# Turning gathered rows by a DMA on f16 halves instead of on TensorE in f32

## The reference, cut to what matters

```python
xn = _layernorm(x)
x = x + gnn(xn, edge_weight, bias, edge_index) + mix(xn, W_qkv, qn_w, kn_w, W_out, b_out)
x = x + ffn(_layernorm(x), norm_scale, gate_w, gate_b, mlp1_w, mlp1_b, mlp2_w, mlp2_b)
...
def ffn(x, ...):                         # E = 8, K = 2, I = 256
    t = x * rsqrt(mean(x * x) + 1e-5) * norm_scale
    top_v, top_i = top_k(t @ gate_w + gate_b, K)
    w = zeros((T, E)).at[arange(T)[:, None], top_i].set(softmax(top_v))
    for e in range(E):
        h = swiglu(t @ mlp1_w[e] + mlp1_b[e])        # (T, 1024) x (1024, 512) -> (T, 256)
        acc += w[:, e:e+1] * (h @ mlp2_w[e] + mlp2_b[e])
    return x + acc
```

## Time and profile before

| | us |
|---|---|
| median of 3 runs | 1025.75 |
| the profiled execution, its time | 1022.55 |
| the profiled execution, its span | 1020.8 |
| PE busy in the span | 922.0 |
| DVE busy | 708.9 |
| ACT busy | 366.5 |
| POOL busy | 173.5 |

### The profile page before, as it was taken

How to read it: one execution, slowest core, us unless ns; L and a number is a source line. 1 busy time by engine, 2 the same in 40 slices (tenths; PEclk the granted TensorE clock), 3 DMA queues, 4 the chain that set the end, 5 groups by cost and what they waited for, 6 DMA issues and landing times.

```text
span 1020.8 us, 16203 instructions
## 1 busy us (share of the span) xinstructions
PE 922.0 (90%) x5361; PEld 576.2 (56%) x5362; DVE 708.9 (69%) x1198; ACT 366.5 (36%) x621; POOL 173.5 (17%) x210
## 2 busy tenths in 40 slices
PE   3998999999999999998998999998359999999992
PEld 2555667766665654555665666665335455555551
DVE  4867999999999974378856777755455455555551
ACT  5657666666441114431122222222112233333331
POOL 1000000000000000015222223322122233323322
PEclk9999999999999999999999999999569999999997
DMA  9735676666663009910255555566459978886544
GB/s 303 227 92 167 201 221 213 194 195 191 213 199 123 22 22 231 336 53 1 61 163 148 159 161 158 151 175 172 177 197 311 315 185 251 270 252 144 123 83 62
DMA packets 89162, 176.59 MB, mean 173 GB/s; under 512 B 24824, under 2 KB 39160, under 8 KB 89088
## 3 DMA queue, kind: packets, MB, share of 16 engines
q1 hardware_dynamic: 81328, 147.50, 46.1%
q0 software_dynamic: 7776, 28.32, 12.4%
HBM read 113.63 MB, written 62.67 MB: 173 GB/s over the span
## 4 chain that ended last, share of the span: by engine, by line
PE 41%; DVE 20%; DMA 18%; ACT 6%; issue 5%; POOL 4%; SPq 3%; DVEq 1%; POOLq 0%; ACTq 0%
PE bank L758 10%; PE windows L1033 9%; DMA arena<-in_w_flat 7%; PE bank L907 7%; DMA arena<-t_dram,arena 6%; PE bank L1051 4%; DVE arena L1687 2%; POOL arena L655 2%; DMA out_x<-arena 2%; DVE arena L1510 2%; PE bank L1024 2%; SPq L541 2%; DMA arena<-in_w_qkv 2%; PE windows L790 2%; DVE arena L1520 2%
## 5 line engine op out<-in xcount | busy, mean ns | idle before, releaser
L758 PE MATMUL bank<-arena 128*125 128x512 f16 x960 | 217.0, 384 | 10.2 <-DVE arena L1483 10.2
L758 PEld LDWEIGHTS bank<-arena 128*125 128x125 f16 x960 | 130.5, 138 | 84.2 <-issue 11.3
L1033 PE MATMUL windows<-arena 128*128 x648 | 149.5, 381 | 0.0
L907 PE MATMUL bank<-arena 128*128 128x416 f16 (+1 forms) x576 | 105.7, 338 | 2.0 <-DMA arena<-split_dram 2.0
L1033 PEld LDWEIGHTS windows<-arena 128*128 128x128 f16 x648 | 63.7, 98 | 65.6 <-issue 1.4
L933 PE MATMUL bank<-arena 128*125 128x512 f16 x432 | 96.3, 379 | 3.8 <-DVE arena L1723 2.3
L939 PE MATMUL bank<-arena 128*125 128x512 f16 x432 | 97.5, 384 | 0.0
L1749 DVE SCALAR_TENSOR_TENSOR arena<-arena 128x512 f16<-128x512 f32 x40 | 39.3, 982 | 61.8 <-ACT arena L1322 61.8
L907 PEld LDWEIGHTS bank<-arena 128*128 128x128 f16 x576 | 55.0, 97 | 45.5 <-DMA arena<-split_dram 2.4
L933 PEld LDWEIGHTS bank<-arena 128*125 128x125 f16 x432 | 58.7, 137 | 37.8 <-DVE arena L1723 2.7
L939 PEld LDWEIGHTS bank<-arena 128*125 128x125 f16 x432 | 59.7, 138 | 34.3 <-issue 1.6
(11 more groups left out here) (248 smaller groups left out, 1428.1 us busy)
## 6 DMA issues: line engine op xcount, KB each, us to landing
arena<-split_dram SPq DMA_DIRECT2D x56, 512.0 KB, 5.5
arena<-in_w_flat SPq DMA_DIRECT2D x44, 512.0 KB, 4.5
split_dram<-arena SPq DMA_DIRECT2D x88, 256.0 KB, 4.6
arena<-in_w_flat SPq DMA_DIRECT2D x40, 256.0 KB, 4.5
split_dram<-arena SPq DMA_DIRECT2D x80, 128.0 KB, 2.3
arena<-in_x SPq DMA_DIRECT2D x20, 448.0 KB
arena<-in_w_qkv SPq DMA_DIRECT2D x8, 1024.0 KB, 11.7
t_dram<-arena SPq DMA_DIRECT2D x10, 448.0 KB
```

The source lines that it names most:

```text
L758: mm = pe.matmul(bank[b][0:TT, :], xt[:, l, k, tok(i)], wkv[:, r, k, c0:c0 + 512], start=(k == 0 and n == 0), stop=(k == KT - 1 and n == 2))
L907: mm = pe.matmul(bank[u % 3][:, 0:n], wq[h][:, l, k, :], xt[:, r, k, a:a + n], start=(k == 0 and c == 0), stop=(k == KT - 1 and c == 2))
L1033: mm = pe.matmul(bank[6][:, :], rowT[s][:, l, k, :], arena16[:, bass.ds(off + (r * KT + k) * 512, 512)], start=(k == 0 and c == 0), stop=( ...
```

## The change

Where tiles of t are stored, they are stored as two f16 halves, high and low, side by side in a row of 2 x 1024 f16 (as many bytes as 1024 f32). ACT makes the high half (`split_hi`) and DVE the low half (`split_lo`) of each of the 10 tiles. SP stores the halves once the low half is there. `tm` in f32 is still what the gate reads.

In the expert stage a gathered row is then already two f16 halves. ACT issues one transposing DMA a block (`turn`), from `rows[s]` (128 rows of 2048 f16) to `rowT[s]` (128 rows of 16 x 128 f16), both in SBUF. PE's 8 transposes, ACT's two copies and DVE's two subtractions of a block are gone. PE's up product waits for the DMA (`turn_in`); POOL's next gather into the same rows buffer waits for it too, where it waited for PE's transposes.

```diff
-    t_dram = scratch("t_dram", [N, D], F32)
+    t_dram = scratch("t_dram", [N, 2 * D], F16)
...
+        t_hl = [view(tail.at + h * 4 * D, [2, D], F16) for h in range(2)]
...
-        rows = [T2([D]) for _ in range(2)]
+        rows = [T2([2 * D], F16) for _ in range(2)]
...
-        rowT = [T2([2, KT, P], F16) for _ in range(2)]
+        rowT = [T2([2 * KT, P], F16) for _ in range(2)]
...
             def store_mixed(i):
                 h = i % 2
-                sp.wait_ge(t_ready, i + 1)
-                tile_dma(sp, t_rows[i], tm[h], t_out[h])
+                sp.wait_ge(t_lo, i + 1)
+                tile_dma(sp, t_rows[i], t_hl[h].rearrange("p a b -> p (a b)"), t_out[h])
...
             with pool.Fori(1, (BLOCKS - 3) // 2) as t:
                 for h in range(2):
-                    pool.wait_ge(rt_psum, 2 * t + h + 1)
+                    pool.wait_ge(turn_in[h], 16 * (t + 1))
                     gather(2 * t + h + 2, h)
                     add_block(2 * t + h - 2, h)
...
-            def row_T(b, s, q):
-
-                pe.wait_ge(row_in[s], 16 * (q + 1))
-                for k in range(KT):
-                    mm = pe.transpose(bank[2 + 2 * s + k // 4][:, (k % 4) * P:(k % 4 + 1) * P], rows[s][:, k * P:(k + 1) * P], ident)
-                mm.then_inc(rt_psum, 1)
-
-            def up(b, s, off, half):
+            def up(b, s, q, off, half):
                 if half == 0:
-                    pe.wait_ge(rt_done, b + 1)
+                    pe.wait_ge(turn_in[s], 16 * (q + 1))
                     pe.wait_ge(h_evac, b)
...
-                if not last:
-                    row_T(b + 1, 1 - s, q + s)
                 pe.wait_ge(expert_ready, need + 1)
-                up(b, s, off, 0)
+                up(b, s, q, off, 0)
...
+            def split_hi(i):
+                h = i % 2
+                a_.wait_ge(t_ready, i + 1)
+                a_.wait_ge(t_out[h], 32 * (i // 2))
+                a_.activation(t_hl[h][0:TT, 0, :], tm[h][0:TT], ACT.Copy).then_inc(t_hi, 1)
...
             for i in range(NT - 2, NT):
                 mix_sqrt(i - 1, 1 - i % 2)
-                for q in quarters(i):
+                for q in quarters(i, 0, 1):
+                    quarter_split(q)
+                split_hi(i - 1)
+                for q in quarters(i, 1):
                     quarter_split(q)
                 tt_copy(i - 1)
             mix_sqrt(NT - 1, 1)
+            split_hi(NT - 1)
             tt_copy(NT - 1)
...
-            def row_hi(b, s, first=False):
-                a_.wait_ge(rt_psum, b + 1)
+            def turn(b, s, q, first=False):
+
+                a_.wait_ge(row_in[s], 16 * (q + 1))
                 if not first:
                     a_.wait_ge(h_mm, b - 1)
-                for q in range(2):
-                    a_.activation(rowT[s][:, 0, 4 * q:4 * q + 4, :], bank[2 + 2 * s + q][:, :].rearrange("p (k n) -> p k n", n=P), ACT.Copy).then_inc(rt_hi, 1)
+                apart(a_)
+                a_.dma_start_transpose(rowT[s], rows[s]).then_inc(turn_in[s], 16)
...
             with a_.Fori(0, (BLOCKS - 3) // 2) as t:
                 for h in range(2):
                     b = 2 * t + h + 2
-                    row_hi(b + 1, 1 - h)
+                    turn(b + 1, 1 - h, t + 1 + h)
                     act_hi(b - 1)
                     scale_y(b - 2, h)
                     sigmoid(b)
...
+            def split_lo(i):
+                v.wait_ge(t_hi, i + 1)
+                v.tensor_tensor(t_hl[i % 2][0:TT, 1, :], tm[i % 2][0:TT], t_hl[i % 2][0:TT, 0, :], ALU.subtract).then_inc(t_lo, 1)
...
             for i in range(NT - 2, NT):
                 mix_norm(i - 1, (i - 1) // 2, 1 - i % 2)
                 gate(i - 3)
-                for q in quarters(i, 0, 3):
+                for q in quarters(i, 0, 1):
+                    quarter_split(q)
+                split_lo(i - 1)
+                for q in quarters(i, 1, 3):
                     quarter_split(q)
...
             mix_norm(NT - 1, NT // 2 - 1, 1)
+            split_lo(NT - 1)
             gate(NT - 3)
             gate(NT - 2)
             gate(NT - 1)
...
-            def row_lo(b, s):
-                for q in range(2):
-                    v.wait_ge(rt_hi, 2 * b + q + 1)
-                    ins = v.tensor_tensor(rowT[s][:, 1, 4 * q:4 * q + 4, :], bank[2 + 2 * s + q][:, :].rearrange("p (k n) -> p k n", n=P),
-                                          rowT[s][:, 0, 4 * q:4 * q + 4, :], ALU.subtract)
-                ins.then_inc(rt_done, 1)
```

More of the change, by code:

```diff
@@ L167, in build_gps_layer @@
         tail = Place(A_AT + 40000, A_AT + 65536)
+        t_hl = [view(tail.at + h * 4 * D, [2, D], F16) for h in range(2)]
         kvn = tail([PAIRS, P])
         kvt = tail([2, PAIRS * P], F16)
+        assert tail.at == A_AT + 40000 + 8 * D
         head_mask = tail([P])
@@ L298, in build_gps_layer @@
         sd2_ready = sem("sd2_ready"); stat2_ready = sem("stat2_ready")
-        t_ready = sem("t_ready")
+        t_ready = sem("t_ready"); t_hi = sem("t_hi"); t_lo = sem("t_lo")
         t_out = [sem(f"t_out{h}") for h in range(2)]
@@ L307, in build_gps_layer @@
         row_in = [sem(f"row_in{h}") for h in range(2)]; idx_ready = sem("idx_ready")
-        rt_psum = sem("rt_psum"); rt_hi = sem("rt_hi"); rt_done = sem("rt_done")
+        turn_in = [sem(f"turn_in{h}") for h in range(2)]
         h_mm = sem("h_mm"); h_evac = sem("h_evac"); glu_ready = sem("glu_ready"); sg_ready = sem("sg_ready")
@@ L711, in _ @@
             for b in range(2):
-                pool.wait_ge(rt_psum, b + 1)
+                pool.wait_ge(turn_in[b], 16)
                 gather(b + 2, b)
@@ L1053, in down, with expert_block @@
                 mm.then_inc(y_mm, 1)
-            def expert_block(b, s, q, first=False, last=False):
+            def expert_block(b, s, q, first=False):
                 off = pe.value_load(blk_i[0:1, bass.ds(b, 1)], min_val=0, max_val=TOP // 2 - 12288)
                 need = pe.value_load(exp_i[0:1, bass.ds(b, 1)], min_val=0, max_val=E)
-                if not last:
-                    row_T(b + 1, 1 - s, q + s)
                 pe.wait_ge(expert_ready, need + 1)
-                up(b, s, off, 0)
+                up(b, s, q, off, 0)
                 if not first:
                     act_T(b - 1)
-                up(b, s, off, 1)
+                up(b, s, q, off, 1)
                 if not first:
@@ L1068, in _ @@
             pe.wait_ge(count_in, 1)
-            row_T(0, 0, 0)
             expert_block(0, 0, 0, first=True)
@@ L1074, in _ @@
             expert_block(BLOCKS - 2, 1, (BLOCKS - 2) // 2)
-            expert_block(BLOCKS - 1, 0, (BLOCKS - 1) // 2, last=True)
+            expert_block(BLOCKS - 1, 0, (BLOCKS - 1) // 2)
             act_T(BLOCKS - 1)
@@ L1330, in _ @@
                 attend_hi(j, 1, PAIRS + j)
+            split_hi(0)
             tt_copy(0)
@@ L1338, in _ @@
                     quarter_split(qs[j - 1])
+                    if j == 1:
+                        split_hi(i - 1)
                     attend_hi(4 * h + j, t + 1, PAIRS * (t + 1) + 4 * h + j)
@@ L1373, in scale_y @@
                 a_.activation(ysb[s], ysb[s], ACT.Copy, scale=p_of[:, bass.ds(b, 1)]).then_inc(y_scaled, 1)
-            row_hi(0, 0, first=True)
-            row_hi(1, 1, first=True)
+            turn(0, 0, 0, first=True)
+            turn(1, 1, 0, first=True)
             sigmoid(0)
-            row_hi(2, 0)
+            turn(2, 0, 1)
             act_hi(0)
@@ L1761, in _ @@
                 add_half(1, 1, half)
+            split_lo(0)
             for i in range(2, NT - 2):
```

14 lines of the change are left out of this document (5 added, 9 removed).

## The result

The changed kernel takes 1129.99 us, the median of 4 runs (1117.13 to 1138.79), beside 1027.37 us for the kernel before in 4 runs on the same chip. The ratio is 1.091, with a 95% interval of 1.084 to 1.099: about 9% slower, where 1045 us, 1.7% more, had been forecast. The profiled execution of after took 1117.13 us with a span of 1115.4.

What follows compares the result with a forecast made beforehand. PE sets the pace in light stretches, with gathers late beside weights; the changed stage was priced by full DMA engines. 16 + 0.5 + 3.5 + 1 = +21 on 1022.55 gave 1043.5, stated as 1045 us; range 1003 to 1150.

Steps and rivals of the forecast that it cites:

- The last step of the sum: Whole kernel: from 1043.5 us for the profiled execution to 1045 us, the median of the runs standing 3.2 us above it.
- the forecast's own signs: Expert stage: DMA share above 0.9 in light stretches and PE idle at the up product's head would confirm the forecast.
- The free transfer: Rival, expert stage: a turn costs 1.4 us with overlapping packet times, PE's savings come back, about 1004 us; chance 0.22.
- the rival of the scatter chain: Expert stage: each scatter waits for the one before, so PE's gain cannot be used; about 1027 us; chance 0.13.
- The loop of a row buffer: Expert stage: gather, turn, then 2.7 us on POOL; 12.2 us for two blocks alone, 20.2 us beside weights.
- the rival of the long turn: Expert stage: a block turned piece after piece, 20 us long without filling the engines; about 1220 us; chance 0.08.
- The turn's price, 2.3 us a block: Expert stage: DMA engine time for 524 KB at the rate of the graph matrix's 256-byte stores; 62 us for 27 blocks.
- the forecast's formula: Expert stage: engine time over a mean share of 0.93, (197 + 62) giving 279 us against 263, +16 us.
- ACT's 0.4 us: Expert stage: ACT's own cost of issuing a turn, taken from SP's 433 ns for a load of as many bytes.
- The first block: Start of the expert stage: a turn of 5 us moves the first up product from 756.03 to 756.5, +0.5 us.
- The gate of tile 7: End of the mix stage: the last low half stands on DVE ahead of this gate, delaying PE's gate product, +3.5 us.
- SP's store of t: Mix stage: the store waits for the low half, and SP's quarter stores and loads follow; +1 us (0 to 7).

Runs made afterwards that it cites:

- after_no_weights: The changed kernel without the weight loads of experts 3 to 7 (products use the weights of the experts three before): 1082.29 us, ratio 1.060 to the kernel before.
- turn_behind: The changed kernel with ACT issuing the turn behind the copy of the activations and the scaling: 1134.08 us, ratio 1.103 to the kernel before.
- before_plus_turn: The kernel before with one unneeded transposing DMA a block added on ACT's queue: 1152.11 us, ratio 1.106 to the kernel before.
- half a turn: The changed kernel turning only the high halves, the low halves being zero: 1079.38 us, ratio 1.054 to the kernel before.
- the small copy: The changed kernel with each turn replaced by two plain DMAs of the same bytes in 256-byte pieces: 1095.45 us, ratio 1.069 to the kernel before.
- the plain copy: The changed kernel with the turn replaced by a plain DMA of the same 524 KB, not turned: 1055.48 us, ratio 1.030 to the kernel before.
- store_late: The changed kernel with SP's store of t issued behind the quarters and the load of the next tile: 1109.54 us.

## Why the prediction was wrong in size

- *What fell short.* The sum had 1043.5 us for the profiled execution, which took 1117.13. Of the 74 us between, 48 lie in the expert stage (64.3 where 16.5 were forecast) and 26 in the mix stage (30.2 where 4.5 were). The last step of the sum is off by 1.7 us besides (1043.5 and 3.2 make 1046.7, not 1045).
- *Direction and mechanism of the expert stage: right in part.* The engines are full in loaded stretches, the mean share is the 0.93 that was taken, and PE waits at the head of the up product for the turn. In light stretches the forecast's own signs failed: a share above 0.9 was named, two of the three shown have 0.81 and 0.86, and PE is busy for 20.00 and 19.30 of 20 us in them. The free transfer is refuted, and so is the rival of the scatter chain, which had no change: PE waits for turns and for the low half, though POOL also waited longer for the scatter before (64.6 us, 45.5 before).
- *The failed step: the turn's length beside weights.* The loop of a row buffer was worked out with a turn of 5 us alone and 8 beside weights, 10.1 us a block, and then left out of the sum, which went by engine time. Beside weights a turn took 22.52 us in after and 25.29 in `after_no_weights`; with 22.5 the forecast's loop gives (9.5 + 22.5 + 2.7) / 2 = 17.4 us a block. Without weights the range is wide: 4.91 us in `turn_behind`, 5.64 to 10.54 in `after_no_weights`, 17.29 in after. The long transfer is mostly a matter of the pieces, not of the turning: the plain copy in 256-byte pieces took 17.16 us beside weights and 7.32 without. So the rival of the long turn, with a chance of 0.08, came true in part, beside weights; but it had the engines not full, and there they were.
- *The turn's price, 2.3 us a block: too low.* It came from packets of 18.1 ns. A packet of the turn costs 28.3 ns here, and a block 3.68 us: 99 us in all, not 62. The price of the pieces was nearly right: plain 256-byte packets cost 19.5 ns in the turn's place and 20.2 beside the kernel before (6.7% of 1056.2 us). What the stores of the earlier trace rows could not show is the price of turning, 24.2 ns a packet in `after_no_weights` (8.0% of 1063.1 us) and 37.8 in `before_plus_turn`.
- *That full engines alone make the sum: wrong.* With 99 us the forecast's formula, (197 + 99) / 0.93 = 318 us, gives 55 of the 64 us; but a stage's length is its engine time over its share whatever the cause, so this proves little. Where the formula is tested it falls short: half a turn, 44 us of engines (4.1% of 1074.4 us), needs 259 us and took 289.1; the small copy, 68 us, needs 285 and took 309.8 at a share of 0.87; the plain copy, 36 us, needs 250 and took 268.4. The length of the transfer stands in PE's chain.
- *ACT's 0.4 us: wrong.* SP's price for issuing as many bytes held for the plain copy (0.47 us) and not for the turn (1.3 to 11.0 us). The text counted a hold of the whole turn to the upper end only; it is where PE's 35.3 us at the down product come from: with the turn issued behind that copy, 2.3 are left (2.2 before the change).
- *The clock: left out.* The granted clock was 0.66 in a loaded stretch with idle spells of PE, and the same products took 21.3 us longer over the stage.
- *The first block: +0.5 forecast.* From gather to first product it is 11.0 us (777.29 to 788.31) where it was 9.0: +2.1.
- *The gate of tile 7: +3.5 forecast, right.* From the issue of the last t to the gate product it was 1.51 us (714.73 to 716.24) and is 5.01 (741.44 to 746.45).
- *SP's store of t: +1 (0 to 7) forecast, some 25 measured.* Order alone gave back 28.3 of the mix stage's 30.2 us, and some 3.5 of those are the gate's. `store_late` gave back 14.2 of them; most of the rest goes with the first tile, whose store came 9.9 us later. The text named the wait and what stands behind it on SP, and then priced it by eight tiles of hand-over. What it missed is that the low half stands on DVE behind the next tile's first work, so the store waits for a step of the next tile, and the quarters and loads of that tile wait for the store, at each of the tiles.
- *The skill's rules.* The Trainium skill, Advanced Engine Details and Errata, section X-Bar Transpose (TRN2), has such transfers as fast as ordinary ones. The trace disagrees: the plain copy of as many bytes takes 3.4% of the engines, 36 us, the turn 99. By the Trainium skill, VectorE: DVE Perf Modes, section The three transpose paths, sixteen turns in a row were an estimate of 20.9 us. The trace does not bear it out: a turn took 4.91 us without weights in `turn_behind`, and came near 20.9 us only beside weights or, once, in the stretch from 1020 us of after.

## What to carry to other kernels

Count a new DMA in packets, not in bytes, and price a packet by a DMA of the same kind: here plain 256-byte packets cost 18 to 20 ns each, and those of a turn 24 to 38. Then ask how long one such transfer takes beside its neighbours, not only what it takes of the engines: that length stands in the chain behind it. Look up how long the issuing engine's queue is held by the same kind of DMA, since everything behind it in that engine's order pays. When a store is made to wait for a later result, follow the queue that issues it one tile further: the loads behind it are the next tile's start.

## What the runs showed that was not expected

A transposing DMA held the queue that issues it for 1.3 to 11.0 us (median 3.1), and for 1.3 to 8.1 us (median 3.7) even without the weights of experts 3 to 7, where a plain copy of the same bytes held it for 0.47 us:

```profile
L1360 ACTq DMA_TRANSPOSE arena<-arena x27: 1334/3655/8082, 779.9 to 1022.8; - x27
```

Cutting the weight loads into four, with the same bytes, made the stage 54 us longer (327.2 to 381.3). And a turn that nothing waits for made the stage longer (383.4 us) than one in the middle of the chain (327.2), where PE also has its row transposes off its hands. The 20 us that the changed kernel loses without the later weights all fall ahead of its first scatter.
